# A layer-normalised graph matmul on one Trainium2 core: VectorE normalises every tile, new orders of the first 16 tiles

## What is computed

```python
mask = adj > 0
head = mask / max(sqrt(sum(mask * mask, axis=-1)), 1e-12)   # per row: 1 / sqrt(number of positive entries)
inc = adj + head
y = x + (inc @ x) / sum(inc, axis=-1)
out = (y - mean(y)) / sqrt(var(y) + 1e-5)                   # along each row of 256
```

## Time and profile before

| | |
|---|---|
| median of 3 runs | 411.33 us (410.71 to 412.14) |
| the profiled execution | 410.89 us |
| its span, first to last instruction | 409.1 us |
| TensorE (PE) busy | 389.3 us, 95% of the span |
| ScalarE (ACT) busy | 371.4 us, 91% |
| VectorE (DVE) busy | 364.2 us, 89% |
| GpSimd (POOL) busy | 346.3 us, 85% |
| granted TensorE clock | 1.0 throughout |

### The profile page before, as it was taken

One profiled execution on the slowest core, in us unless ns is written; L12 is line 12 of the kernel. 1 busy time (PEld: TensorE's weight loads), 2 busy tenths in 40 slices (PEclk: granted clock), 3 DMA queues, 4 the chain that ended last, 5 costly groups with the idle time before them and its releaser, 6 DMA issues.

```text
span 409.1 us, 8775 instructions
## 1 busy us (share of the span) xinstructions
PE 389.3 (95%) x2224; PEld 343.1 (84%) x2224; DVE 364.2 (89%) x757; ACT 371.4 (91%) x507; POOL 346.3 (85%) x222
## 2 busy tenths in 40 slices
PE   1689999999999999999999999999999999999995
PEld 0668889988888878888888888888888888888884
DVE  0897999999999999999999999999999999999932
ACT  4967999999999999999999999999999999998530
POOL 3111599999999999999999999999999999999970
PEclk9999999999999999999999999999999999999999
DMA  8999997576677667667666665767666666670020
GB/s 237 269 253 253 264 261 215 168 238 204 200 221 222 190 187 215 190 206 222 200 208 205 195 205 191 208 216 214 197 210 201 196 206 192 215 218 27 27 64 13
DMA packets 36183, 80.00 MB, mean 196 GB/s; under 512 B 9536, under 2 KB 17728, under 8 KB 36160
## 3 DMA queue, kind: packets, MB, share of 16 engines
q1 hardware_dynamic: 35776, 78.68, 66.1%
q10 hardware_dynamic: 384, 1.05, 0.8%
HBM read 75.50 MB, written 4.19 MB: 195 GB/s over the span
## 4 chain that ended last, share of the span: by engine, by line
PE 83%; POOL 4%; issue 4%; SPq 4%; DMA 3%; DVE 1%; ACT 1%; POOLq 0%; ACTq 0%
PE edge L1307 46%; PE edge L1321 23%; PE edge L1258 12%; POOL inc_split L564 3%; DMA x_stage<-in_x_dram 3%; SPq L156 3%; PE sums L1253 1%; SPq L179 1%; DVE incT L767 1%; POOL inc_split L578 0%; PE sums L1232 0%; SPq L184 0%; POOL small L548 0%; DVE inc L751 0%; ACT scaled L251 0%
## 5 line engine op out<-in xcount | busy, mean ns | idle before, releaser
L564 POOL TENSOR_TENSOR inc_split<-incT,inc_split 128x960 fp32r<-128x960 f32 x120 | 269.4, 2272 | 2.4 <-ACT inc_split L262 0.5
L1307 PE MATMUL edge<-x_split,inc_split 128*128 128x512 f32 (+1 forms) x930 | 223.4, 392 | 0.1
L1307 PEld LDWEIGHTS edge<-x_split,inc_split 128*128 128x128 f32 x930 | 168.1, 188 | 32.8 <-ACT inc_split L262 0.9
L751 DVE SCALAR_TENSOR_TENSOR inc<-raw,scaled 128x1024 f32<-128x1024 f32 x128 | 154.3, 1206 | 3.3 <-ACT scaled L251 2.4
L767 DVE STREAM_TRANSPOSE incT<-inc 128x1024 f32<-128x1024 f32 x128 | 156.3, 1230 | 0.7 <-PE edge L1258 0.4
L251 ACT ACTIVATE scaled<-raw,small 128x1024 f32<-128x1024 f32 x128 | 141.1, 1107 | 2.8 <-DVE inc L751 1.2
L240 ACT ACTIVATE sign_out<-raw 128x1024 int8<-128x1024 f32 x128 | 133.7, 1045 | 4.5 <-DMA raw<-in_adj_dram 4.3
L1321 PEld LDWEIGHTS edge<-x_split,inc_split 128*128 128x128 f32 x900 | 112.2, 191 | 2.3
L1321 PE MATMUL edge<-x_split,inc_split 128*128 128x256 f32 x900 | 113.5, 283 | 0.0
L262 ACT CAST inc_split<-incT 128x960 fp32r<-128x960 f32 x90 | 86.5, 984 | 0.7 <-DVE incT L767 0.7
L583 POOL TENSOR_TENSOR small<-small 128x1 f32<-128x1 f32 x24 | 13.2, 554 | 37.2 <-DVE small L733 37.0
(11 more groups left out here) (42 smaller groups left out, 138.8 us busy)
## 6 DMA issues: line engine op xcount, KB each, us to landing
raw<-in_adj_dram SPq DMA_DIRECT2D x504, 128.0 KB, 2.5
rows<-in_x_dram SPq DMA_DIRECT2D x32, 128.0 KB, 2.1
out_dram<-rows SPq DMA_DIRECT2D x32, 128.0 KB, 1.7
x_stage<-in_x_dram SPq DMA_DIRECT2D x12, 256.0 KB, 9.4
raw<-in_adj_dram ACTq DMA_DIRECT2D x8, 128.0 KB, 5.1
x_stage<-in_x_dram SPq DMA_DIRECT2D x4, 192.0 KB, 13.6
x_native<-in_x_dram SPq DMA_DIRECT2D x4, 64.0 KB, 5.7
```

The lines of the kernel that those rows point to most:

```text
L564: nc.gpsimd.tensor_tensor(lo_of(s, q), incT[:, s, 0:SPLIT, q, :], hi_of(s, q).bitcast(fp32), ALU.subtract).then_inc(lo_by_pool, 1)
L751: nc.vector.scalar_tensor_tensor(inc[:, q, :], raw[:, s, q, :], 0.0, scaled[q % 2][:, :], ALU.is_gt, ALU.add, accum_out=part_sums[:, s, 0, ...
L1307: last = nc.tensor.matmul(edge[s][:, c0:c1], inc_split[s][:, 0, b, :, :].rearrange("p q j -> p (q j)"), x_split[:, b, :, :].rearrange("p h ...
```

## The change

ScalarE's `normalise` is removed, and so is `shift_of` on VectorE. In its place VectorE runs `finish_rows`, the instruction of L826 (`tensor_scalar` of 128 x 256, in and out of SBUF), for tiles 0 to 30; tile 31 keeps `normalise_last`. In the loop and in the last four tiles `finish_rows` stands exactly where `shift_of` stood, and the rest of their order is kept. Tiles 14 and 15 are taken out of the loop and written out, and the written-out lists of ScalarE, VectorE, GpSimd and TensorE for the first 16 tiles get another order. The list of the sync queue is not touched. The diff, cut to its core (the written-out lists of tiles 0 to 6 are reordered in the same manner and left out):

```diff
@@ -266,11 +264,6 @@
                 act.wait_ge(x_in[c], FOUR_DMAS)
                 nc.scalar.copy(x_part(c, 0), x_staged(c)).then_inc(x_hi_by_act, 1)
 
-            def normalise(t, s):
-                act.wait_ge(shift_ready, t - 3)
-                nc.scalar.activation(y[:, s, :], y[:, s, :], ACT.Identity, scale=norm_rstd[:, s, G:G + 1],
-                                     bias=shift[:, s:s + 1]).then_inc(result_ready, 1)
...
-            sign_quarter(14, 0, 7, 1)
-            normalise(9, 1)
             scale_quarter(13, 1, 1)
             round_quarter(12, 0, 3)
             sign_quarter(14, 0, 7, 2)
+            sign_quarter(14, 0, 7, 3)
             scale_quarter(13, 1, 2)
-            sign_quarter(14, 0, 7, 3)
             scale_quarter(13, 1, 3)
+            round_quarter(13, 1, 0)
             sign_quarter(15, 1, 7, 0)
-            round_quarter(13, 1, 0)
+            scale_quarter(14, 0, 0)
             sign_quarter(15, 1, 7, 1)
-            scale_quarter(14, 0, 0)
             scale_quarter(14, 0, 1)
-            normalise(10, 0)
             round_quarter(13, 1, 2)
             round_quarter(13, 1, 3)
-            with act.Fori(7, PAIRS - 2) as u:
+            sign_quarter(15, 1, 7, 2)
+            scale_quarter(14, 0, 2)
+            sign_quarter(15, 1, 7, 3)
+            scale_quarter(14, 0, 3)
+            sign_quarter(16, 0, 8, 0)
+            round_quarter(14, 0, 0)
+            sign_quarter(16, 0, 8, 1)
+            scale_quarter(15, 1, 0)
+            scale_quarter(15, 1, 1)
+            round_quarter(14, 0, 2)
+            round_quarter(14, 0, 3)
+            sign_quarter(16, 0, 8, 2)
+            scale_quarter(15, 1, 2)
+            sign_quarter(16, 0, 8, 3)
+            scale_quarter(15, 1, 3)
+            sign_quarter(17, 1, 8, 0)
+            round_quarter(15, 1, 0)
+            sign_quarter(17, 1, 8, 1)
+            scale_quarter(16, 0, 0)
+            scale_quarter(16, 0, 1)
+            round_quarter(15, 1, 2)
+            round_quarter(15, 1, 3)
+            with act.Fori(8, PAIRS - 2) as u:
                 scale_quarter(2 * u, 0, 2)
                 sign_quarter(2 * u + 1, 1, u, 2)
                 sign_quarter(2 * u + 1, 1, u, 3)
@@ -461,7 +469,6 @@
                 scale_quarter(2 * u + 1, 1, 0)
                 sign_quarter(2 * u + 2, 0, u + 1, 1)
                 scale_quarter(2 * u + 1, 1, 1)
-                normalise(2 * u - 3, 1)
                 round_quarter(2 * u, 0, 2)
                 round_quarter(2 * u, 0, 3)
                 scale_quarter(2 * u + 1, 1, 2)
@@ -473,7 +480,6 @@
                 scale_quarter(2 * u + 2, 0, 0)
                 sign_quarter(2 * u + 3, 1, u + 1, 1)
                 scale_quarter(2 * u + 2, 0, 1)
-                normalise(2 * u - 2, 0)
                 round_quarter(2 * u + 1, 1, 2)
                 round_quarter(2 * u + 1, 1, 3)
...
             norm_of(13, 1)
-            round_quarter(12, 0, 1)
             low_quarter(12, 0, 0)
             low_quarter(12, 0, 1)
             low_quarter(12, 0, 2)
             low_quarter(12, 0, 3)
             norm_of(14, 0)
+            low_quarter(13, 1, 0)
             round_quarter(13, 1, 1)
-            low_quarter(13, 1, 0)
             low_quarter(13, 1, 1)
             low_quarter(13, 1, 2)
             low_quarter(13, 1, 3)
-            with pool.Fori(7, PAIRS - 2) as u:
+            round_quarter(14, 0, 1)
+            norm_of(15, 1)
+            low_quarter(14, 0, 0)
+            low_quarter(14, 0, 1)
+            low_quarter(14, 0, 2)
+            low_quarter(14, 0, 3)
+            norm_of(16, 0)
+            round_quarter(15, 1, 1)
+            low_quarter(15, 1, 0)
+            low_quarter(15, 1, 1)
+            low_quarter(15, 1, 2)
+            low_quarter(15, 1, 3)
+            with pool.Fori(8, PAIRS - 2) as u:
                 norm_of(2 * u + 1, 1)
...
@@ -818,14 +830,6 @@
                 nc.vector.tensor_scalar(count_var[:, s, G:G + 1], mean_var[:, s, 1:2], EPS, None,
                                         ALU.add).then_inc(var_ready, 1)
 
-            def normalise_by_dve(t, s):
-                if t < EARLY - 4:
-                    dve.wait_ge(rstd_ready, t + 1)
-                else:
-                    dve.wait_ge(norm_ready, t + 5 - EARLY)
-                nc.vector.tensor_scalar(y[:, s, :], y[:, s, :], mean_var[:, s, 0:1], norm_rstd[:, s, G:G + 1],
-                                        ALU.subtract, ALU.mult).then_inc(result_ready, 1)
-
             def y_last(t, s, u):
 
                 dve.wait_ge(hi_used, t - FIRST_SPLIT + 1)
@@ -848,135 +852,135 @@
                 nc.vector.tensor_scalar(y[:, s, :], y[:, s, :], mean_var[:, s, 0:1], norm_rstd[:, s, G:G + 1],
                                         ALU.subtract, ALU.mult).then_inc(last_ready, 1)
 
-            def shift_of(t, s, alone=0):
+            def finish_rows(t, s, alone=0):
 
                 if alone:
                     dve.wait_ge(rstd_ready, alone)
                 else:
                     dve.wait_ge(norm_ready, t + 5 - EARLY)
...
@@ -987,31 +991,31 @@
             inverse_degree(5, 1)
             transpose_quarter(7, 1, 1)
             y_first(5, 1, 2)
+            inc_quarter(7, 1, 2)
             count_of(8, 0)
-            inc_quarter(7, 1, 2)
             y_second(5, 1)
+            inc_quarter(7, 1, 3)
             transpose_quarter(7, 1, 2)
-            inc_quarter(7, 1, 3)
-            shift_of(4, 0)
+            statistics(5, 1)
+            finish_rows(4, 0)
             transpose_quarter(7, 1, 3)
-            statistics(5, 1)
             inc_quarter(8, 0, 0)
             mean_variance(5, 1)
             transpose_quarter(8, 0, 0)
             variance_eps(5, 1)
+            inc_quarter(8, 0, 1)
             degree(6, 0)
-            inc_quarter(8, 0, 1)
-            inverse_degree(6, 0)
             inc_quarter(8, 0, 2)
             transpose_quarter(8, 0, 1)
+            inverse_degree(6, 0)
             transpose_quarter(8, 0, 2)
             y_first(6, 0, 3)
             count_of(9, 1)
             y_second(6, 0)
             inc_quarter(8, 0, 3)
             statistics(6, 0)
-            shift_of(5, 1)
             transpose_quarter(8, 0, 3)
+            finish_rows(5, 1)
             mean_variance(6, 0)
             inc_quarter(9, 1, 0)
             variance_eps(6, 0)
@@ -1021,44 +1025,44 @@
             inc_quarter(9, 1, 1)
             inc_quarter(9, 1, 2)
             y_first(7, 1, 3)
-            y_second(7, 1)
             count_of(10, 0)
             transpose_quarter(9, 1, 1)
             inc_quarter(9, 1, 3)
+            finish_rows(6, 0)
             transpose_quarter(9, 1, 2)
-            shift_of(6, 0)
+            y_second(7, 1)
+            transpose_quarter(9, 1, 3)
             statistics(7, 1)
-            transpose_quarter(9, 1, 3)
+            inc_quarter(10, 0, 0)
             mean_variance(7, 1)
...
@@ -1072,14 +1076,14 @@
             degree(10, 0)
             transpose_quarter(12, 0, 1)
             inverse_degree(10, 0)
+            inc_quarter(12, 0, 3)
             count_of(13, 1)
             y_first(10, 0, 5)
             transpose_quarter(12, 0, 2)
+            transpose_quarter(12, 0, 3)
             y_second(10, 0)
-            inc_quarter(12, 0, 3)
-            shift_of(9, 1)
+            finish_rows(9, 1)
             statistics(10, 0)
-            transpose_quarter(12, 0, 3)
             inc_quarter(13, 1, 0)
             mean_variance(10, 0)
             inc_quarter(13, 1, 1)
@@ -1088,18 +1092,52 @@
             transpose_quarter(13, 1, 0)
             inverse_degree(11, 1)
             transpose_quarter(13, 1, 1)
-            inc_quarter(13, 1, 2)
             y_first(11, 1, 5)
             count_of(14, 0)
+            inc_quarter(13, 1, 2)
+            y_second(11, 1)
             inc_quarter(13, 1, 3)
-            y_second(11, 1)
-            shift_of(10, 0)
             statistics(11, 1)
             transpose_quarter(13, 1, 2)
+            finish_rows(10, 0)
             mean_variance(11, 1)
             transpose_quarter(13, 1, 3)
             variance_eps(11, 1)
-            with dve.Fori(7, PAIRS - 2) as u:
+            inc_quarter(14, 0, 0)
+            degree(12, 0)
+            inc_quarter(14, 0, 1)
+            inverse_degree(12, 0)
+            transpose_quarter(14, 0, 0)
+            y_first(12, 0, 6)
+            inc_quarter(14, 0, 2)
+            transpose_quarter(14, 0, 1)
+            y_second(12, 0)
+            count_of(15, 1)
+            inc_quarter(14, 0, 3)
+            statistics(12, 0)
+            transpose_quarter(14, 0, 2)
+            transpose_quarter(14, 0, 3)
+            mean_variance(12, 0)
+            finish_rows(11, 1)
+            inc_quarter(15, 1, 0)
+            variance_eps(12, 0)
+            degree(13, 1)
+            inc_quarter(15, 1, 1)
+            inverse_degree(13, 1)
+            transpose_quarter(15, 1, 0)
+            y_first(13, 1, 6)
+            inc_quarter(15, 1, 2)
+            y_second(13, 1)
```

(40 more changed lines are left out.)

251 lines of the change are left out of this document (114 added, 137 removed).

## The result

The changed kernel takes 426.49 us in the median (425.06 to 427.56, 4 runs) against 411.02 for the kernel before beside it. The ratio is 1.036, with a 95% interval from 1.031 to 1.040. It is slower, by 15.5 us; forecast were 434.0 us and a range of 420 to 439. The profiled execution took 426.97 us, its span is 425.0 us, 15.9 more than before.

What follows compares the result with a forecast made beforehand. TensorE's matmuls, tile after tile, were taken to bound the kernel. 4.5 + 18.6 - 0.5 + 0 = +22.6 us on the profiled 410.89 us gave 433.5, as median 434.0 us; range 420 to 439, the forecast's own 430 to 439.

Steps and rivals of the forecast that it cites:

- rival (a): Loop: VectorE and GpSimd meet as by chance, 1.07 us left per wait; +10.0 us, 421.3 us in all; chance 0.14.
- part 2: Nine written-out normalisations, tiles 4 to 12: waits of 9.5 us less 4.96 us of VectorE idle time, net +4.5 us.
- the period: Time per loop tile: from 11.55 to 12.79 us, 1.24 more, with VectorE as the bound.
- the number of tiles: Steps between count_of for tile 16 and for tile 31: 15 at 1.24 us, 18.6 us in all.
- part 3: The other orders, from the start to the kernel's end: 0 us, between -0.5 and +1.5.
- ScalarE's 0.5: ScalarE without its normalisation ends the two roundings that release the next tile's hi matmuls sooner: -0.5 us once.
- The wait of one instruction: Loop: finish_rows waits out GpSimd's low_quarter, 1.91 us left, and ends 0.15 us behind it; VectorE 1.89 us later per tile.
- It has 0.65 us of idle time to give: Loop: VectorE's idle time per tile, 0.65 us, is taken off the 1.89 us by which it gets later.
- The 1.86 us of stalls cannot be won where VectorE is the bound: From 125.32 to 208.03 us: TensorE's chain holds 1.86 us of stalls over seven tiles, which better orders would not win back.
- Fewer warm-ups ... move nothing: Start, to 54.0 us: fewer warm-ups and other places of the small sums cost 0, between -0.5 and +1.5 us.
- The rule that was weighed: Written-out tiles: any GpSimd instruction blocks, norm_of and round_quarter included, 1.39 us counted in; 1.4 us less if only L564 blocked.
- (b): Loop: finish_rows slips in before low_quarter and GpSimd waits; period stays 11.55 us, 409.4 us in all; chance 0.06.

Runs made afterwards that it cites:

- move-only kernel: The kernel before with its old orders everywhere; only the normalisation moves, finish_rows in each place of shift_of and ScalarE's normalise gone: 430.64 us, ratio 1.044.
- The kernel without the waits: The changed kernel with a PSUM shift and scalar_tensor_tensor as finish_rows for tiles 4 to 28, 6 and 8 placed later, plus eleven warm-up matmuls: 410.34 us, ratio 0.997.
- the kernel where only tiles 6 and 8 waited: The changed kernel with finish_rows as PSUM shift and scalar_tensor_tensor in tiles 4 to 28 except 6 and 8: 412.94 us, with eleven warm-up matmuls 412.93.
- the changed kernel with warm-ups: The changed kernel with eleven warm-up matmuls put back on TensorE around sum_early(1, 2), nothing else: 427.82 us.
- the kernel with the swap: The changed kernel with finish_rows one place earlier, ahead of the fourth transpose, in the loop and in tiles 28 to 30: 414.86 us, ratio 1.007.
- the old orders and the PSUM form: The kernel before without ScalarE's normalise; VectorE does a PSUM shift and scalar_tensor_tensor instead (tiles 8, 29, 30: tensor_scalar): 411.24 us, ratio 0.998.

## Why the prediction was right or wrong

The direction, the mechanism and the place in the loop were right. The 426.5 us lie in the range of 420 to 439, but only because it was stretched down to rival (a); they lie 3.5 us below 430 to 439, the forecast's own range. (Its lower end was set with 0.5 us for part 2, though the text bounds that part at 0.) Forecast were 22.6 us on top of the profiled execution before, and the spans show 15.9, so 6.7 too many. They are made up of part 2 (3.2 too many), the period (13 x 0.20 = 2.6) and the number of tiles (2 x 1.24 = 2.5), against which stand part 3 (1.1 too few) and ScalarE's 0.5. That the last two were off the other way was luck.

**The wait of one instruction: right.** Forecast were 1.91 us left in the loop and an end 0.15 us behind low_quarter; measured, 1.90 to 1.92 and 0.15, ten times in a row. The pattern held itself, as argued: GpSimd's norm_of still starts 0.3 us behind the late count_of. ScalarE idles 15.4 us in 11 tiles, 1.4 us a tile.

**The period: 12.61 us, forecast 12.79.** The step that failed is "It has 0.65 us of idle time to give". Both tiles counted from their count_of (223.37 before, 289.16 now), VectorE's position after the wait was 1.89 us later and stayed so up to the transpose ahead of y_first; it was 1.74 at y_first, then 1.71, and 1.06 at the next count_of. So VectorE had 0.15 us of slack ahead of y_first, of which the timeline before shows only 0.07 as idle, and another 0.64 ahead of count_of, where it shows 0.56. The missing 0.08 at each place are the overlap with which VectorE's instructions otherwise follow one another. VectorE gave 0.83 us, and with 1.89 - 0.83 the period grows by 1.06. (The last two of the tiles take 12.51 us, which makes it 1.04 on average.)

**The number of tiles: 13, forecast 15.** The changed kernel was locked only from TensorE's tile 17 on. The normalisation of tile 12 met 0.84 us and that of tile 13 only 0.16 us of GpSimd's work, since VectorE came out of the written-out part with another distance to GpSimd than the loop's. Rows of the kernel before could not show that distance. The move-only kernel, which keeps their orders, is locked earlier, with 1.9 us left at each normalisation from tile 12's on, and there the 15 tiles from TensorE's 15 to 30 did lose, 189.0 us for 173.2. 13 x 1.04 = 13.6 us stand against the 18.6 forecast.

**Part 2: +1.3 us, forecast +4.5.** This is the largest of the five. That the waits exist was right: the nine met between 0.11 and 1.58 us left, 7.0 in sum for the 9.64 forecast. But neither sum is a price. The kernel without the waits puts it at 3.0 us from tile 8 to 15. About half of that comes from one wait: tile 6 met round_quarter with 0.11 us left (0.12 forecast) and still took 2.48 us. In the kernel where only tiles 6 and 8 waited, 1.5 of the 2.45 us were lost by TensorE's tile 10, ahead of tile 8's wait. Against the 3.0 stand the 1.7 us of stalls that are gone with the new orders and ScalarE's work; "The 1.86 us of stalls cannot be won where VectorE is the bound" was wrong for this part.

**Part 3: +1.1 us, forecast 0.** "Fewer warm-ups ... move nothing" was wrong for the profiled execution: the clock fell, and tile 8 started 1.1 us later, 0.1 later where the clock did not fall (the changed kernel with warm-ups). It was inside the bounds given (-0.5 to +1.5). An execution also adds its own chance here: the kernel with the swap has the same list up to tile 8 and started it at 127.08 us in place of 126.24, with the clock's first entry at 21.3 us in place of 17.4.

**The rule that was weighed** (GpSimd's other instructions block too) is shown for round_quarter: in the kernel with the swap fifteen normalisations end 0.15 us behind one. No normalisation met norm_of, so that stays open.

The rivals: (a), chance meetings, describes the written-out part and the first two loop tiles, not the loop. (b), finish_rows first, did happen, for tile 13 at 0.37 us, but did not last. The -0.5 us for ScalarE does not show in the changed kernel, whose TensorE waited for ScalarE's signs in the loop and not for its roundings; with the old orders and the PSUM form up to 0.4 us of it may be there.

## What to carry to other kernels

A VectorE instruction that needs the port it shares with GpSimd cost what was left of GpSimd's instruction, not its own duration. Where GpSimd waits for VectorE once per iteration, as in this loop, both keep step and the same wait comes back every time: read from the trace what GpSimd is doing at that place, and move the instruction by one (11.6 of 15.5 us here) or write it in a form whose second tensor comes from PSUM (13.6 of them, and all of them where the last waits went too). An engine's idle time must be taken where its position slips, since part of it lies inside the recorded durations.
